# Edge weights moved from the coefficients to the one-hot tile, and 28 blocks gathered ahead

## The reference

```python
x_n = _layernorm(x)
w_full = einsum('rb,bdo->rdo', w_comp, weight)     # 16 edge types from 8 bases
x_rel = einsum('nd,rdo->rno', x_n, w_full)
msg = x_rel[etypes, src] * norm                    # norm: edge_weight1, one number for each edge
agg = segment_sum(msg, dst, num_segments=6250)
x = x + relu(agg + h_bias + x_n @ loop_weight)
# then x + layernorm(moe(layernorm(x))), two of 16 experts for each node
```

## Time and profile before

| | us |
|---|---|
| median of three runs | 2823.43 (2821.42 to 2824.64) |
| the profiled execution | 2827.04, its span 2825.3 |
| TensorE matmul busy | 2229.5 (79%) |
| TensorE weight load busy | 1855.0 (66%) |
| GpSimd busy | 1813.0 (64%) |
| VectorE busy | 952.7 (34%) |
| ScalarE busy | 591.0 (21%) |
| the 3920 matmuls of the steps (L1181) | 1062.2 |
| granted TensorE clock, mean | 0.907 |

### The profile page before, as it was taken

One profiled execution on the slowest core, in us unless ns is written; L12 is line 12 of the kernel. 1 busy time (PEld: TensorE's weight loads), 2 busy tenths in 40 slices (PEclk: granted clock), 3 DMA queues, 4 the chain that ended last, 5 costly groups with the idle time before them and its releaser, 6 DMA issues. The chain is left out here.

```text
span 2825.3 us, 40400 instructions
## 1 busy us (share of the span) xinstructions
PE 2229.5 (79%) x11563; PEld 1855.0 (66%) x11564; DVE 952.7 (34%) x2141; ACT 591.0 (21%) x1382; POOL 1813.0 (64%) x2001
## 2 busy tenths in 40 slices
PE   1666665766777877887899899899998279999987
PEld 0455444644655665676677777778786269999975
DVE  6762111121212212222223332322322853333348
ACT  2100000100111111121222232232322012233345
POOL 0467777777777777777777777777760035555544
PEclk9788777887979988999999999999999689999998
DMA  6363333343434433444444444444440722222256
GB/s 227 98 193 105 105 104 104 104 122 104 119 116 124 119 116 115 116 136 118 120 121 132 123 126 123 122 131 119 129 108 26 242 74 70 69 71 69 70 165 238
DMA packets 146259, 338.57 MB, mean 120 GB/s; under 512 B 36674, under 2 KB 56290, under 8 KB 146051
## 3 DMA queue, kind: packets, MB, share of 16 engines
q0 software_dynamic: 89296, 245.33, 29.9%
q1 hardware_dynamic: 39311, 59.54, 6.2%
q10 hardware_dynamic: 17588, 32.88, 3.5%
HBM read 292.84 MB, written 47.97 MB: 121 GB/s over the span
## 5 line engine op out<-in xcount | busy, mean ns | idle before, releaser
L981 POOL DMA_INDIRECT rows<-feat,idx x1526 | 1451.2, 951 | 450.0 <-issue 436.6
L1181 PE MATMUL psW<-rows,S 128*128 x3920 | 1062.2, 434 | 361.6 <-SPq L944 329.3
L1181 PEld LDWEIGHTS psW<-rows,S 128*128 128x128 f32 x3920 | 842.9, 219 | 576.3 <-issue 439.1
L1060 DVE TENSOR_TENSOR S<-psHere,coefS 128x896 f32<-128x896 f32 x280 | 303.2, 1090 | 1390.5 <-PE psW L1181 1385.8
L1239 ACT COPY z<-psW 128x512 f32<-128x512 f32 x196 | 114.9, 586 | 1366.8 <-PE psW L1181 1364.3
L1146 PE MATMUL psG<-wb,zT 128*128 128x256 f32 (+1 forms) x1600 | 353.5, 379 | 0.0
L1146 PEld LDWEIGHTS psG<-wb,zT 128*128 128x128 f32 (+1 forms) x1600 | 300.6, 188 | 44.7
L1566 PE MATMUL psH<-xT,w1x 128*128 128x128 f32 x1840 | 226.7, 277 | 0.4 <-DVE w1x L1608 0.2
L1517 POOL DMA_INDIRECT expert_rows<-os,at_rows x114 | 113.9, 999 | 171.3 <-DVE os L1624 171.3
L1566 PEld LDWEIGHTS psH<-xT,w1x 128*128 128x128 f32 x1840 | 216.1, 193 | 2.5 <-issue 2.5
L1575 PE MATMUL psO<-w2s,hT 128*128 x912 | 215.7, 379 | 0.0
(11 more groups left out here) (254 smaller groups left out, 1370.1 us busy)
## 6 DMA issues: line engine op xcount, KB each, us to landing
rows<-feat,idx POOLq DMA_INDIRECT x1568
g<-expert_rows SPq DMA_DIRECT2D x24, 512.0 KB, 6.0
w1s<-in_L_ffn_w SPq DMA_DIRECT2D x8, 1024.0 KB, 10.8
w2s<-in_L_ffn_w SPq DMA_DIRECT2D x16, 512.0 KB, 10.8
feat<-rows SPq DMA_DIRECT2D x24, 256.0 KB, 4.6
fts<-feat ACTq DMA_DIRECT2D x24, 256.0 KB
h<-in_x ACTq DMA_DIRECT2D x24, 256.0 KB
y_rows<-y ACTq DMA_DIRECT2D x24, 256.0 KB
```

What stands on the lines that cost most here:

```text
L981: e.indirect_dma_start(rows[:, at * H:(at + 1) * H], None, d.feat, bass.IndirectOffsetOnAxis(ap=idx[:, q * GB + u:q * GB + u + 1], axis=0) ...
L1060: e.tensor_tensor(S[h0 + h][:, :].rearrange("p (s b n) -> p s b n", s=U, b=B), both[:, h * U:(h + 1) * U, :].unsqueeze(2).to_broadcast([P, ...
L1181: e.matmul(psW[:, bass.ds(bank[u], H)], S[h][:, u * ZC:(u + 1) * ZC], rows[:, bass.ds(slot[u], H)], start=False, stop=True, skip_group_che ...
```

## The change

- `EG` is 2, not 3: GpSimd gathers 28 blocks ahead in `expand`, two behind each of the last 8 edge gathers, and the graph layer starts with the 29th.
- In `expand` the coefficients are no longer multiplied by the weights. VectorE's `weigh` is gone; ScalarE copies `psC` out unchanged (`coefs`), with the same waits, once for each part, behind `group` and `types` in its loop.
- In the graph layer VectorE multiplies the compared tile `both` by the weights, in place in PSUM, once for each pair of turns, and waits for the comparison ahead of it. The multiply into `S` waits for that.
- `wgtS` (7936 bytes in each partition) lives through the graph layer.

```diff
-EG = RB // GB - 1
+EG = 2
...
                 if g >= GR:
-                    for j in range(3 * (g - GR), 3 * (g - GR + 1)):
+                    for j in range(EG * (g - GR), EG * (g - GR + 1)):
                         ahead(j)
-            for j in range(3 * (SG - GR), EG * GB):
+            for j in range(EG * (SG - GR), EG * GB):
                 ahead(j)
...
+            def coefs(n):
+                e.wait_ge(s_pc, n + 1)
+                if n >= NEAR + DL:
+                    e.wait_ge(s_lst[n % DL], late_before(n))
+                e.copy(coefs_at(n), psC[n % 2][:, 0:GN]).then_inc(s_co, 1)
+
             types(0)
             for n in range(total):
                 g, q = divmod(n, NQ)
...
                 if q == 1 and g + 1 < SG:
                     types(g + 1)
+                coefs(n)
...
-            def weigh(n):
-                e.wait_ge(s_tc, n // NQ + 1)
-                e.wait_ge(s_pc, n + 1)
-                if n >= NEAR + DL:
-                    e.wait_ge(s_lst[n % DL], late_before(n))
-                e.tensor_tensor(coefs_at(n).rearrange("p (s b) -> p s b", b=B), psC[n % 2][:, 0:GN].rearrange("p (s b) -> p s b", b=B),
-                                wgtS[:, n * CS:(n + 1) * CS].unsqueeze(2).to_broadcast([P, CS, B]), ALU.mult).then_inc(s_co, 1)
...
-                if n >= 1:
-                    weigh(n - 1)
-            weigh(total - 1)
...
                 e.tensor_tensor(both, dstS[:, bass.ds(turn * U, 2 * U)].unsqueeze(2).to_broadcast([P, 2 * U, WIN]),
-                                node_h.unsqueeze(1).to_broadcast([P, 2 * U, WIN]), ALU.is_equal).then_inc(s_hot, 2)
+                                node_h.unsqueeze(1).to_broadcast([P, 2 * U, WIN]), ALU.is_equal).then_inc(s_hot, 1)
+                e.wait_ge(s_hot, turn + 1)
+                e.tensor_tensor(both, both, wgtS[:, bass.ds(turn * U, 2 * U)].unsqueeze(2).to_broadcast([P, 2 * U, WIN]), ALU.mult).then_inc(s_hot, 1)
...
+        wgtS = sb("wgtS", [P, SC])
...
-            wgtS = far("wgtS", [P, SC])
```

More of the change, by code:

```diff
@@ L885, in _, with graph_layer @@
             e.tensor_scalar(ident[:, :], ident_i[:, :], 0.0, None, ALU.is_equal)
-def graph_layer(nc, d, a, ctl, pairs, room, wend, srcT, dstS, coefS, ident, wb, lw, hb, gw, s_w, logit, mean, rstd, idx, rows, s_row):
+def graph_layer(nc, d, a, ctl, pairs, room, wend, srcT, dstS, wgtS, coefS, ident, wb, lw, hb, gw, s_w, logit, mean, rstd, idx, rows, s_row):
     from contextlib import ExitStack
@@ L1842, in gnn @@
         wb, lw, hb, gw = sb("wb", [P, HC, B, H]), sb("lw", [P, HC, H]), sb("hb", [P, H]), sb("gw", [P, HC, X])
-        graph_layer(nc, d, a, ctl, pairs, room, wend, srcT, dstS, coefS, ident, wb, lw, hb, gw, s_w, logit, mean, rstd, idx, rows, s_row)
+        graph_layer(nc, d, a, ctl, pairs, room, wend, srcT, dstS, wgtS, coefS, ident, wb, lw, hb, gw, s_w, logit, mean, rstd, idx, rows, s_row)
 def program(nc, a, out):
```

## The result

The changed kernel takes 2828.37 us (median of 20 runs, 2825.60 to 2831.64), the kernel before 2822.65 us in the runs beside it (20 runs, 2819.36 to 2828.05). The ratio is 1.0020 (95% interval 1.0014 to 1.0026): slower by 5.7 us. The forecast was slower by 10.9 us, in a range of 2826.0 to 2840.0 us: the direction and the range held, the size was about twice what was measured.

The account below looks back on a forecast made before the run. GpSimd's train of row gathers was taken to bound the kernel. Fourteen gathers moved behind its hole cost 17.64 us, less 6.7 us of shorter `expand`: 10.9 us on 2823.4, 2834.3 us, range 2826.0 to 2840.0.

Parts of the forecast that it names:

- The bound: GpSimd's train of row gathers sets the pace; TensorE's last real wait for rows is at 1738.18 us.
- X: Displacement of the gather train, and so of the kernel's end: 17.64 us less what `expand` gets shorter, forecast 10.9 us later.
- Fourteen gathers, 17.64 us: Fourteen gathers move from before the train's hole at the start of the graph layer to behind it, costing 17.64 us.
- The loop of `expand`: Without VectorE's multiply, a loop between engines takes 3.44 us for four steps instead of 4.16; ScalarE's copy 0.38 us, hidden.
- The first half: First 31 steps of `expand`, straight into `coefS`: forecast gain 5.0 us.
- The multiply in the graph layer: VectorE's 140 new multiplies of 0.40 us, 0.67 us more for two turns; hidden, cost 0.
- rival D: The new multiply reaches TensorE in the last tiles: 6 us on top of the forecast, 2840 us; chance 0.05.
- The second half: Last 31 steps of `expand`, through four buffers stored to DRAM: 33.9 us instead of 35.6, a gain of 1.7 us.
- rival B: Stores stop holding buffers as gathers sharing the DMA engines end earlier: `expand` 13.9 us shorter, 2821 to 2827 us; chance 0.20.
- D: What `expand` gets shorter: 5.0 us in its first half plus 1.7 in its second, 6.7 us; bounds 5.0 and 13.9.
- A: The forecast itself: end 10.9 us later, 2834.3 us, or 7.6 to 12.6 us later; chance 0.60.
- Rival C: ScalarE's copy and order, or the stores, eat the gain: `expand` 0 to 4 us shorter, 2837 to 2841 us; chance 0.13.

Follow-up runs that it names:

- no_mul: Changed kernel without the multiply by the edge weights in the graph layer: 2828.15 us, ratio 1.0022 to the kernel before.
- the second profile: Profile of the kernel before, run once more without an edit: span 2820.4 us, one run of 2822.19 us.
- dl8: Changed kernel with eight instead of four `late` buffers between `expand` and its stores: 2825.54 us, ratio 1.0013 to the kernel before.
- eg3: Changed kernel with 42 blocks gathered ahead instead of 28 (EG = 3): 2818.89 us, ratio 0.9990 to the kernel before.
- old_eg2: Kernel before with only 28 blocks gathered ahead, the multiply still on VectorE in `expand`: 2835.88 us, ratio 1.0049 to the kernel before.
- wait_vec: Changed kernel with VectorE also waiting for a free `late` buffer, behind the `hot` of the step after: 2829.19 us, ratio 1.0030 to the kernel before.
- again: Changed kernel run once more without an edit: 2828.45 us, ratio 1.0024 to the kernel before.
- eg3_dl8: Changed kernel with 42 blocks gathered ahead and eight `late` buffers: 2818.23 us, ratio 0.9987 to the kernel before.

## Why the prediction was right in direction and wrong in size

**The bound: right.** "Whatever moves the train by X us moves the end by X us" is borne out by the table over 18 us and on both sides of zero: shift and time differ by at most 0.7 us in its eight rows of 2818 to 2836 us. Where the train lets go was read wrong: everything behind 1738.18 was said to be TensorE's own work, but the turn at 1783 us waits for rows in five of ten profiles. The rule holds all the same, since both turns hang on the same train.

**Fourteen gathers, 17.64 us: right** (17.61).

**The loop of `expand`: right.** The group of four was summed to 3.44 us. ScalarE's rows in the changed kernel show it:

```profile
120.38 0.27 ACT L742 CAST dstS<-psT 128x128 bf16<-128x128 f32 x1
...
123.81 0.27 ACT L742 CAST dstS<-psT 128x128 bf16<-128x128 f32 x1
...
127.25 0.27 ACT L742 CAST dstS<-psT 128x128 bf16<-128x128 f32 x1
```

123.81 - 120.38 = 3.43 us and 127.25 - 123.81 = 3.44 us. The copy on ScalarE was put at 0.38 us by columns and took 0.372. The first half went from 32.3 us to between 26.7 and 27.6, a gain of about 5 as forecast.

**The multiply in the graph layer: right** in price (0.40 us) and in cost (none that can be told); rival D, 6 us on top, is refuted by no_mul.

**The second half: the step that failed.** I forecast a gain of 1.7 us, and it was 5.8 to 6.8 against the second profile (34.8 us before, 28.0 to 29.0 after), 6.6 to 7.6 against the first (35.6). The sum was 26.7 for the loop, 3.4 for the old stalls, 2.8 for their growth at the faster pace and 1 for new ones: 33.9 us. By its own count that is 7.2 us of stalls; the runs show 2.3 to 3.3 us over the bare loop. What is wrong in it:
- The count. From the first copy to the last are 30 intervals, not 31, so the loop is 25.75 us (dl8), 0.95 us less. The same slip stood in the old stalls, 35.6 - 31.2 = 4.4 us and not 3.4, so the two nearly cancel (34.0 instead of 33.9 us), and the stalls were in truth put at 8.2 us.
- The stores beside the gathers. With 42 gathers ahead the stalls are 31.8 - 25.75 = 6.0 us (eg3), with 28 they are 2.3 to 3.3 us. This is about 3 to 4 us, the larger part of the miss, and the step that failed: fewer gathers beside the stores were taken to change nothing. I named it as rival B and argued it away with the stall at 177.46, which came when the last gather had been issued 4 us before. That argument was wrong: the store in question was issued at 172.5, while the gathers' queue still moved packets until 175 us (81 of them, above). One late stall says nothing of the stores that come 15 us after the last gather: in old_eg2 there is no stall behind 157.52.
- Who waits. The wait for a store left VectorE's queue, where `hot` stood behind it, for ScalarE's. I counted the copy's price in the new queue but not what no longer stands behind its wait. wait_vec's one profile puts that at 1.6 to 2.6 us of the half; in the time it isn't clear of noise. The first profile's late stores (35.6 against 34.8) are another 0.8 us of the forecast.

What I put in as growth of the stalls was not foolish: in eg3, with the gathers as before, the stalls are 6.0 us against 34.8 - 31.2 = 3.6 us at the old pace (30 x 1.04 = 31.2).

**D and X.** D was forecast at 6.7 and is 177.54 - 165.33 = 12.2 us (10.5 in no_mul, 11.6 in again), so X = 17.6 - 12.2 = 5.4 us, where the 43rd gather shows 5.3. Against the profile that I had, D is 179.22 - 165.33 = 13.9 us and X 3.7 us, rival B's numbers to the tenth. But the time rose by 5.7 us, because that profile stood late. So the truth lies between A and B: B's mechanism was at work, but stores still held ScalarE 9 times for 6.8 us, and B's mark (the 43rd gather before 187 us) was missed by 0.3 us. Rival C, that `expand` would gain 0 to 4 us, is refuted.

**The Trainium skill's rule.** By the rows of old_eg2 a store of 128 KB lands in 1.7 us when the gathers are over and in 3.3 us beside them. The Trainium skill (DMA: Bandwidth & Descriptors, Anatomy of one DMA) gives a fit of 2.0 us and bytes at 436 GB/s, an estimate of 2.3 us for 128 KB. That section is on DMAs issued by GpSimd, which the prediction did not say, and these stores are SyncE's. Neither measured figure is 2.3 us: it is less when the gathers are over and more beside them, and it is the figure beside the gathers that decides whether four buffers are enough.

**What the change is worth in its parts.** Where the gathers ahead stay at 42, the new `expand` brings 2.8 us (eg3; interval 0.3 to 5.4). Going from 42 to 28 ahead costs 9.6 us in the new `expand` (eg3 to again) and 14.2 us in the old one (old_eg2). The first part alone beats both kernels, as does eg3_dl8. Why it brings 3 us and not its full 8.3 us of shorter `expand` (177.54 to 169.21) is the restart behind GpSimd's own last gather.

## What to carry to other kernels

Find the train that sets the pace and convert every edit into its displacement; here that gave the time of kernels from 2818 to 2836 us within 0.7 us. Look for its last wait in more than one profile: the one read here laid the last one on "issue". When work is taken off a shared queue, price the waits of everything that shared it (here stores at 3.3 and 1.7 us), and when a wait moves to another engine, look at what stood behind it in the old queue. And take the reference positions from more than one profile if the difference sought is a few us: here one profile alone was off by 4 us.

## What was not expected

- The pace of the gathers is not quite constant between executions of the same kernel: from the 43rd to the last, 1922.9 us in the first profile of before and 1919.6 us in the second, for the same instructions. In the other profiles of the table it was 1918.4 to 1920.7 us.
- The restart of the train behind a block depends on what GpSimd did last. Behind an `expand` that ends late, it is 4.3 to 4.5 us from the last copy to the first gather (165.33 to 169.65; the earlier trace rows: 179.22 to 183.58). Behind its own gathers it is 7.7 us from the 42nd to the 43rd, of which 5.1 us are idle before the iota. What it waits for in these 5.1 us stays open.
- In four of the experiments the kernel before was 31% slower (3700.22 against 2822 us). Their traces have gaps called "issue" in front of TensorE's turns and a slower `expand`, while a gather next to another kept its 1.25 us. Nothing in these runs shows why.
